# Attention inside a macaron layer: heavy and light key halves take turns within an item, and the values' products come in twos

## The chip, the core and the metric

The kernel runs on one core of a Trainium2 chip. The metric is device microseconds of one execution, the median of several runs. PE is TensorE (its weight loads are listed as PEld), DVE is VectorE, ACT is ScalarE, POOL is GpSimd, SP issues DMAs.

## What is computed

A macaron layer over 16 sequences of 512 rows of 128 values: half a feed-forward layer with routed experts, attention, and half a feed-forward layer again. The change is in attention alone, of which this much matters:

```python
q, k, v = proj(Wq, bq), proj(Wk, bk), proj(Wv, bv)              # 16 heads of 8 values
dist = clip(arange(s)[:, None] - arange(s)[None, :], -128, 128) + 128
scores = einsum('bhqd,bhkd->bhqk', q, k)
scores = scores + einsum('bhqd,qkd->bhqk', q, rel_emb[dist])    # relative positions, clipped at 128
attn = softmax(scores / sqrt(8), axis=-1)
local_ctx = einsum('bhqk,bhkd->bhqd', attn, v)
# a global, linear part (sigma_q, M, z) is mixed in with a gate, then the output projection
```

Within 128 positions the relative term differs from key to key; beyond that it is one number per query on each side. So only blocks of 128 keys next to the block of 128 queries, or equal to it, need a table added; the others get their term inside the score product.

## The kernel before

**Items and steps.** Attention works through 128 items. An item is one sequence (16), one set of four heads (4) and one half of the queries (2 blocks of 128): `half_of(c)` is c % 2, eight items make a sequence (`PER`). The queue of each engine is written out slot by slot, `slot(c)` with four steps k = 0 to 3, and each slot works on several items at once: raw scores of item c + 2, the band product of item c + 4, turned scores of item c.

**One step on PE** (L1437 to L1457), in this order:
- `scores(c + 2, k)` (L1240): for two heads, 128 queries by 512 keys into `ps_s`, for DVE's row maximum (L1838), which adds the table `rel` on the way. A score bank is written again one step later, when its maximum is taken (`max_done`). The heads are the pair 1 - k%2.
- `band_product(c + 4, k)` (L1256): queries by 256 relative positions for the pair k%2. ACT copies it out (L1481), POOL sends it to HBM (L1575, L1577), SP fetches it back skewed into `rel` (L1751). The copies of k = 0 and 2 wait until the transfer of the item before, out of the same half of `src`, has landed.
- `scores_turned(c, k)` (L1212): keys by queries, for two heads and one half of the keys (two blocks of 128), into the two banks of `ps_t`. Each bank waits until ACT has taken the exponential of the step before out of it (`exp_done`).
- `add_turned(c, k)` (L1225): turns the blocks of `rel` and adds them in PSUM, for adjacent blocks only. Of the four pairs of a key block and a query block in a step, all four are adjacent where keys and queries are the same half (8 additions for two heads: a heavy step), and one is where they are not (2 additions: a light step).
- On some steps work of other stages in the bank `misc`: the turn of the maxima (L1312, every k = 0), projections (L1368, L1374, L1390, L1433), groups of four transposes (L1322, L1334, L1407, L1428), smaller products (L1343, L1351, L1382, L1421). Their places (slot in the sequence, k) are fixed in constants.
- `values(..., kb)` (L1270): the products of probabilities and values for one block of 128 keys and four heads, 8 instructions in the trace (two passes each).

**The order of the steps.** `scores_turned` takes key half k // 2 and head pair k % 2. For even items the half of the keys at k = 0 and 1 is the half of the queries, for odd ones it is that at k = 2 and 3: heavy, heavy, light, light, and then light, light, heavy, heavy. The products of the first two key blocks stand behind k = 2 and 3, those of the last two behind k = 0 and 1 of the next slot.

**The others.** ACT per step: the copy of the band product, then two exponentials (L1472), then now and then a copy of a projection. DVE per step: what is due of `maxima_out` (k = 1, L1848), `values_out` (k = 2, L1856), projections, `GLOBAL_OUT` and the like, `route_low` (L2073); then two maxima; then small steps of the router.

Of the kernel before, what the change touches and what calls it, by code (L numbers as in the profile page):

```python
# [5 lines left out]
P = 128  # L6
# [955 lines left out]
def attention_phase(nc, io, X, STATS, tables, rows):  # L962
# [4 lines left out]
    QPB = 4  # L967
    S = QPB * P
    B = Q // QPB
    HG = 4  # L970
# [45 lines left out]
    with ExitStack() as ctx:  # L1016
# [6 lines left out]
        def ring(name, per):  # L1023
            return Ring(ctx.enter_context(nc.semaphore(f"at_{name}")), per)
# [67 lines left out]
        m_turned, m_row = ring("m_turned", 1), ring("m_row", 1)  # L1092
        m_in = [ring(f"m_in{r}", 16) for r in range(R2)]
        t_done, exp_done = ring("t_done", 2 * HG), ring("exp_done", 2 * HG)
        pv_done, oc_done = ring("pv_done", QPB), ring("oc_done", 1)
        o_turned, o_step = ring("o_turned", QPB), ring("o_step", 2 * QPB)
        g_prod, g_step = ring("g_prod", 2), ring("g_step", 6)
        mixed_done, mixed_turned, mixedT_done = (ring(x, 1) for x in ("mixed_done", "mixed_turned", "mixedT_done"))
# [68 lines left out]
        def set_of(c):  # L1167
            return c % PER // 2

        def par_of(c):  # L1170
            return c // PER % R2

# [25 lines left out]
        def _(pe):  # L1198
            def scores_turned(c, k):

                j, r, s, kp, hp = c, par_of(c), set_of(c), k // 2, k % 2
                if k == 0:
                    m_ring, n = pair_ring(m_in, c)
                    pe.wait_ge(m_ring.sem, m_ring.at(n, 16))
                for i in range(2):
                    h = 2 * hp + i
                    exp_done.wait(pe, j, 2 * k + i - 1)
                    rows = slice(32 * h, 32 * h + ROW + 1)
                    q = qs[rows, r, s, HALF * half_of(c):HALF * (half_of(c) + 1)]
                    for n in range(2):  # L1210
                        kb = 2 * kp + n
                        pe.matmul(ps_t[:, i, HALF * n:HALF * (n + 1)], ks[rows, r, s, kb * P:(kb + 1) * P], q,  # L1212
                                  start=(n == 0), stop=False, skip_group_check=True)

            def add_turned(c, k):

                kp, hp = k // 2, k % 2
                for i in range(2):
                    for n in range(2):
                        kb = 2 * kp + n  # L1220
                        for l in range(2):
                            qb = 2 * half_of(c) + l
                            if kb < qb - 1 or kb > qb + 1:
                                continue
                            ins = pe.matmul(ps_t[:, i, HALF * n + P * l:HALF * n + P * (l + 1)],  # L1225
                                            rel[:, c % RREL, l, 2 * hp + i, kb * P:(kb + 1) * P], ident[:],
                                            start=False, stop=True, is_transpose=True, skip_group_check=True)
                    ins.then_inc(t_done.sem, 1)

# [26 lines left out]
                    ins = pe.matmul(ps_r[:, i, 0:BAND], qs[rows, r, s, rows_of(c, l)], rs[rows, :], start=True, stop=True)  # L1256
                ins.then_inc(qr_done.sem, 1)

            def values(c, kb):

                j, r, s = c, par_of(c), set_of(c)
                pe.wait_ge(exp_done.sem, exp_done.at(j, HG * (kb // 2 + 1)))
                if kb == 0:
                    oc_done.wait(pe, j, 0)
                    if c % PER == 0:
                        b = c // PER
                        pe.wait_ge(v_done.sem, v_done.at(b, 1))
                for g in range(HG):
                    at = (HG * s + g) * (HD + 1)
                    ins = pe.matmul(ps_v[32 * g:32 * g + 32, 0:HALF], v[:, r, kb, at:at + 32],  # L1270
                                    probs[:, kb // 2, g, kb % 2, :], start=(kb == 0), stop=(kb == QPB - 1),
                                    skip_group_check=True)
                ins.then_inc(pv_done.sem, 1)

            def maximum_left(c):
# [160 lines left out]
            def slot(c):  # L1436
                for k in range(4):  # L1437
# [13 lines left out]
                        project(c, k)  # L1451
                    if leaving(c) is not None:
                        leave(c, k)
                    if k < 2 and item(c - 1) is not None:
                        values(c - 1, 2 + k)
                    elif k >= 2 and item(c) is not None:
                        values(c, k - 2)  # L1457
            for c in SLOTS:
                slot(c)

# [1 line left out]
        def _(act):  # L1462
            def exponent(c, k):

                j, kp, hp = c, k // 2, k % 2
                if k == 0:
                    pv_done.wait(act, j, 2 - QPB)
                elif k == 2:
                    pv_done.wait(act, j, 0)
                for i in range(2):  # L1470
                    act.wait_ge(t_done.sem, t_done.at(j, 2 * k + i + 1))
                    act.activation(probs[:, kp, 2 * hp + i].rearrange("p n q -> p (n q)"), ps_t[:, i, :],  # L1472
                                   ACT.Exp).then_inc(exp_done.sem, 1)

            def band_out_of_psum(c, k):
# [346 lines left out]
        def _(dve):  # L1822
# [27 lines left out]
            def values_out(c):  # L1850

                j, b = c, leaving(c)
                dve.wait_ge(pv_done.sem, pv_done.at(j, QPB))
                if c % PER < 2 and b is not None:
                    dve.wait_ge(o_turned.sem, o_turned.at(b, 2 * (c % PER) + 2))
                dve.tensor_copy(oc[:, 2 * half_of(c):2 * half_of(c) + 2, set_of(c), :],  # L1856
                                ps_v[:, 0:HALF].rearrange("p (t q) -> p t q", t=2)).then_inc(oc_done.sem, 1)
# [550 lines left out]
```

## Time and profile before

| | |
|---|---|
| median of 3 runs | 2129.41 us (2128.08 to 2130.55) |
| the profiled execution | 2133.66 us, its span 2131.9 us |
| attention, first to last scores on PE | 451.4 to 1745.1 us of the span |
| PE / DVE / ACT / POOL busy | 91% / 71% / 64% / 60% of the span |
| mean granted TensorE clock | 0.934 of 2.4 GHz |

The rest of the span is the two feed-forward layers. In the timeline a row is a run of like instructions: where the first starts, how long the run takes until its last one ends, the engine, the line, what is written from what, how many, and in brackets the idle time of the engine just before. Matmuls overlap, so the time of a stage on PE is read from the start of its row to the start of the next. A step of PE goes from the start of one row of L1240 to the start of the next.

### The profile page before, as it was taken

The page shows a single profiled execution, that of the slowest core. Times are in us where ns is not written, and L with a number is a line of the kernel's source. Part 1 is how long each engine was busy: PE and PEld are TensorE (multiplying, and loading weights), DVE is VectorE, ACT ScalarE, POOL GpSimd, SP SyncE. Part 2 cuts the span into 40 slices and gives each one's busy share as a digit, 9 for nine tenths or more (in the row PEclk, how much of TensorE's full clock was granted, in tenths as well). Part 3 has the DMA queues.
Part 4 walks back from the last instruction along what each step waited for, and adds up shares of the span by engine and source line. Part 5 has one row for each costly group of instructions (what it writes and reads, how often), then busy time and mean ns, then how long its engine had stood idle before and what let it go on. Part 6 is the DMA issues. An engine that isn't in the chain of part 4 may idle for free. (4 is left out here: it accounts for less than half of the span.)

```text
span 2131.9 us, 47704 instructions
## 1 busy us (share of the span) xinstructions
PE 1947.8 (91%) x15256; PEld 1345.7 (63%) x15256; DVE 1507.4 (71%) x4387; ACT 1370.2 (64%) x2645; POOL 1272.4 (60%) x1806
## 2 busy tenths in 40 slices
PE   4779999769999999999999999999999996899992
PEld 3667788535666666665666666666666664688882
DVE  7987667646767767777767677777777664876775
ACT  3767677536766766667766666766766652667771
POOL 0777217346656656776766667666676442637775
PEclk9999999859999989899989999999999897999996
DMA  5457889688989888888888888888888751277757
GB/s 145 170 206 265 290 258 307 197 214 253 255 236 263 238 233 255 217 240 255 231 241 240 220 249 253 238 247 240 238 256 239 212 150 62 82 234 265 256 194 253
DMA packets 291741, 484.75 MB, mean 227 GB/s; under 512 B 42724, under 2 KB 198500, under 8 KB 291492
## 3 DMA queue, kind: packets, MB, share of 16 engines
q1 hardware_dynamic: 234612, 298.65, 49.2%
q0 software_dynamic: 54144, 181.91, 26.5%
q8 instruction: 124, 2.03, 0.4%
q10 hardware_dynamic: 2736, 1.13, 0.2%
q14 instruction: 125, 1.02, 0.2%
HBM read 245.23 MB, written 208.89 MB: 213 GB/s over the span
## 5 line engine op out<-in xcount | busy, mean ns | idle before, releaser
L1838 DVE CUSTOM_DVE_ANT_0 at_junk<-at_ps_s,at_rel 128x512 bf16<-128x512 f32 x1024 | 664.2, 686 | 190.7 <-PE at_ps_s L1240 166.4
L1472 ACT ACTIVATE at_probs<-at_ps_t 128x512 f32<-128x512 f32 x1024 | 559.1, 599 | 81.9 <-PE at_ps_t L1225 70.6
L1481 ACT COPY at_src<-at_ps_r 128x512 f32<-128x512 f32 x512 | 302.0, 590 | 376.5 <-PE at_ps_r L1256 265.6
L1225 PE MATMUL at_ps_t<-tab_ident,at_rel 128*128 128x128 f32 x2560 | 412.3, 294 | 0.0
L1270 PE MATMUL at_ps_v<-at_probs,at_v 128*32 128x256 f32 x4096 | 340.8, 406 | 0.2 <-ACT at_probs L1472 0.2
L1240 PE MATMUL at_ps_s<-at_ks,at_qs 31*128 31x512 f32 x1024 | 326.2, 515 | 11.3 <-DVE at_mx L1838 6.2
L1225 PEld LDWEIGHTS at_ps_t<-tab_ident,at_rel 128*128 128x128 f32 x2560 | 284.8, 146 | 72.2 <-issue 9.1
L1240 PEld LDWEIGHTS at_ps_s<-at_ks,at_qs 31*128 31x128 f32 x1024 | 124.8, 188 | 267.0 <-DVE at_mx L1838 150.6
L1212 PE MATMUL at_ps_t<-at_qs,at_ks 32*128 32x256 f32 x2048 | 271.3, 300 | 5.1 <-DMA at_qs<-at_mrow 2.2
L645 POOL DMA_INDIRECT rows_x<-ffn_sent_or_back,rows_index x160 | 168.1, 1051 | 145.3 <-ACT ffn_sent_or_back L596 97.7
L912 DVE TENSOR_TENSOR ffn_h<-ffn_silu,ffn_ps_gate 128x512 f32<-128x512 f32 x234 | 160.4, 686 | 129.5 <-ACT ffn_silu L615 129.1
L615 ACT ACTIVATE ffn_silu<-ffn_ps_mid 128x512 f32<-128x512 f32 x234 | 139.5, 596 | 173.3 <-PE ffn_ps_gate L443 173.3
L1256 PE MATMUL at_ps_r<-tab_rs,at_qs 31*128 31x256 f32 x1024 | 205.4, 398 | 22.5 <-ACT at_src L1481 15.8
L1212 PEld LDWEIGHTS at_ps_t<-at_qs,at_ks 32*128 32x128 f32 x2048 | 207.8, 194 | 26.2 <-ACT at_probs L1472 19.5
L1575 POOL DMA_DIRECT2D at_band<-at_src x192 | 142.3, 741 | 108.6 <-POOL at_src L1568 107.1
L652 POOL DMA_INDIRECT rows_t<-ffn_y,ffn_row_ids x156 | 152.3, 977 | 79.5 <-issue 45.4
L1567 POOL COPY at_far<-at_src 128x4 f32<-128x4 f32 x192 | 37.0, 193 | 233.9 <-ACT at_src L1481 233.6
L850 DVE TENSOR_TENSOR ffn_h_lo<-ffn_h,ffn_h_hi 128x512 fp32r<-128x512 f32 x234 | 160.2, 685 | 0.1
L1270 PEld LDWEIGHTS at_ps_v<-at_probs,at_v 128*32 128x32 f32 x4096 | 82.3, 110 | 103.3 <-issue 53.9
L561 ACT CAST ffn_h_hi<-ffn_h 128x512 fp32r<-128x512 f32 x234 | 143.2, 612 | 2.6 <-DVE ffn_h L912 2.6
L443 PE MATMUL ffn_ps_mid<-ffn_xT_hi,ffn_w_expert 128*128 128x512 f32 x340 | 135.9, 400 | 5.5 <-issue 3.6
L1856 DVE COPY at_oc<-at_ps_v 128x256 f32<-128x256 f32 x128 | 54.2, 423 | 120.6 <-PE at_ps_v L1270 120.5
(295 smaller groups left out, 3775.8 us busy)
## 6 DMA issues: line engine op xcount, KB each, us to landing
at_band<-at_src POOLq DMA_DIRECT2D x192, 574.0 KB
at_rel<-at_band SPq DMA_DIRECT2D x512, 143.5 KB
ffn_w_expert<-rows_w SPq DMA_DIRECT2D x85, 768.0 KB, 4.7
at_band<-at_src POOLq DMA_DIRECT2D x64, 512.0 KB
ffn_xg<-rows_x SPq DMA_DIRECT2D x46, 256.0 KB
rows_y<-ffn_y SPq DMA_DIRECT2D x46, 256.0 KB, 5.8
ffn_xg<-rows_x SPq DMA_DIRECT2D x39, 258.0 KB
at_rel<-at_band SPq DMA_DIRECT2D x64, 128.0 KB
```

Of the source, the lines that this page charges most:

```text
L645: pool.indirect_dma_start(to, bass.IndirectOffsetOnAxis(index[:, t // PAIR, k, t % PAIR * T + s, :], 0), xe[:, i % RX, k, s, :], None).the ...
L652: pool.indirect_dma_start(rows.t, bass.IndirectOffsetOnAxis(row_ids[:, b % RI, c, :], 0), y[:, b % RY, c, :], None).then_inc(z_out[b % RY] ...
L850: dve.tensor_tensor(h_lo[:, u % RH, :], h[:, u % RH, :], h_hi[:, u % RH, :].bitcast(F32), ALU.subtract).then_inc(hlo_done, 1)
L912: dve.tensor_tensor(h[:, u % RH, :], silu[:, u % RH, :], ps_gate[:, u % 2, :], ALU.mult).then_inc(h_done, 1)
L1212: pe.matmul(ps_t[:, i, HALF * n:HALF * (n + 1)], ks[rows, r, s, kb * P:(kb + 1) * P], q, start=(n == 0), stop=False, skip_group_check=True)
L1225: ins = pe.matmul(ps_t[:, i, HALF * n + P * l:HALF * n + P * (l + 1)], rel[:, c % RREL, l, 2 * hp + i, kb * P:(kb + 1) * P], ident[:], sta ...
L1240: pe.matmul(ps_s[:, i, :], qs[rows, r, s, rows_of(c, l)], ks[rows, r, s, :], start=True, stop=True).then_inc(s_done.sem, 1)
L1256: ins = pe.matmul(ps_r[:, i, 0:BAND], qs[rows, r, s, rows_of(c, l)], rs[rows, :], start=True, stop=True)
L1270: ins = pe.matmul(ps_v[32 * g:32 * g + 32, 0:HALF], v[:, r, kb, at:at + 32], probs[:, kb // 2, g, kb % 2, :], start=(kb == 0), stop=(kb == ...
L1472: act.activation(probs[:, kp, 2 * hp + i].rearrange("p n q -> p (n q)"), ps_t[:, i, :], ACT.Exp).then_inc(exp_done.sem, 1)
L1481: act.copy(src[:, l, 2 * hp:2 * hp + 2, 0:BAND], ps_r[:, :, 0:BAND]).then_inc(qr_out.sem, 1)
L1838: dve.tensor_tensor_reduce(out=junk[:, i, :], in0=ps_s[:, i, :], in1=rel[:, c % RREL, l, h, :], scale=1.0, scalar=-3e38, op0=ALU.add, op1= ...
```

## The change

Within an item, the steps now go through one pair of heads and both halves of the keys, then through the other pair. `unit` gives the half of the keys and the head: the half of the queries first (heavy), then the other (light). The half `k % 2` of `probs` now holds heavy or light steps. The products are called twice an item, each time for both blocks of a key half: those of the heavy steps behind k = 3, those of the light ones behind k = 0 of the next slot. `pv_done` counts two an item instead of four, and the waits on it follow. The exponentials of k = 0 and k = 1 wait for the products of the item before that read the same half of `probs`.

```diff
+        def unit(c, k, i):
+            return (half_of(c) + k) % 2, 2 * (k // 2) + i
...
             def scores_turned(c, k):
-                j, r, s, kp, hp = c, par_of(c), set_of(c), k // 2, k % 2
+                j, r, s = c, par_of(c), set_of(c)
...
                 for i in range(2):
-                    h = 2 * hp + i
+                    kp, h = unit(c, k, i)
                     exp_done.wait(pe, j, 2 * k + i - 1)
...
             def add_turned(c, k):
-                kp, hp = k // 2, k % 2
                 for i in range(2):
+                    kp, h = unit(c, k, i)
...
-            def values(c, kb):
+            def values(c, part):
                 j, r, s = c, par_of(c), set_of(c)
-                pe.wait_ge(exp_done.sem, exp_done.at(j, HG * (kb // 2 + 1)))
-                if kb == 0:
+                pe.wait_ge(exp_done.sem, exp_done.at(j, 2 * HG - 2 + 2 * part))
+                if part == 0:
                     oc_done.wait(pe, j, 0)
...
-                for g in range(HG):
-                    at = (HG * s + g) * (HD + 1)
-                    ins = pe.matmul(ps_v[32 * g:32 * g + 32, 0:HALF], v[:, r, kb, at:at + 32],
-                                    probs[:, kb // 2, g, kb % 2, :], start=(kb == 0), stop=(kb == QPB - 1),
-                                    skip_group_check=True)
+                for n in range(2):
+                    for g in range(HG):
+                        kp, _ = unit(c, part, 0)
+                        at = (HG * s + g) * (HD + 1)
+                        ins = pe.matmul(ps_v[32 * g:32 * g + 32, 0:HALF], v[:, r, 2 * kp + n, at:at + 32],
+                                        probs[:, part, g, n, :], start=(part == 0 and n == 0), stop=(part == 1 and n == 1),
+                                        skip_group_check=True)
                 ins.then_inc(pv_done.sem, 1)
...
-                    if k < 2 and item(c - 1) is not None:
-                        values(c - 1, 2 + k)
-                    elif k >= 2 and item(c) is not None:
-                        values(c, k - 2)
+                    if k == 0 and item(c - 1) is not None:
+                        values(c - 1, 1)
+                    elif k == 3 and item(c) is not None:
+                        values(c, 0)
...
             def exponent(c, k):
-                j, kp, hp = c, k // 2, k % 2
-                if k == 0:
-                    pv_done.wait(act, j, 2 - QPB)
-                elif k == 2:
-                    pv_done.wait(act, j, 0)
+                j = c
                 for i in range(2):
+                    _, h = unit(c, k, i)
                     act.wait_ge(t_done.sem, t_done.at(j, 2 * k + i + 1))
-                    act.activation(probs[:, kp, 2 * hp + i].rearrange("p n q -> p (n q)"), ps_t[:, i, :],
+                    if i == 0 and k < 2:
+                        pv_done.wait(act, j, k - 1)
+                    act.activation(probs[:, k % 2, h].rearrange("p n q -> p (n q)"), ps_t[:, i, :],
                                    ACT.Exp).then_inc(exp_done.sem, 1)
...
             def values_out(c):
-                dve.wait_ge(pv_done.sem, pv_done.at(j, QPB))
+                dve.wait_ge(pv_done.sem, pv_done.at(j, 2))
```

## Rows read from the trace of the kernel before

**Rows 1.** The page: busy us, share, instructions; then one costly group (busy, mean ns).

```profile
PE 1947.8 (91%) x15256; PEld 1345.7 (63%) x15256; DVE 1507.4 (71%) x4387; ACT 1370.2 (64%) x2645; POOL 1272.4 (60%) x1806
...
L1270 PE MATMUL at_ps_v<-at_probs,at_v 128*32 128x256 f32 x4096 | 340.8, 406 | 0.2 <-ACT at_probs L1472 0.2
```

**Rows 2.** Windows: stretch, length, busy us by engine, PEclk, DMA share, GB/s.

```profile
521.00:1702.10 1181.10, 1152.78 (x10846) 732.19 (x10843) 844.90 (x2786) 795.90 (x1490) 781.89 (x1273) 0.95 0.85 241
...
1427.60:1446.10 18.50, 18.00 (x145) 11.58 (x141) 10.19 (x33) 10.57 (x20) 11.55 (x20) 0.72 0.77 216
```

**Rows 3.** The tile of the scores: durations min/median/max in ns, first and last start.

```profile
L1240 PE MATMUL at_ps_s<-at_ks,at_qs x1024: 488/497/792, 451.4 to 1745.1; 31*128 31x512 f32 x171
```

**Rows 4.** Timeline of PE from 562.71 to 567.31: two heavy steps.

```profile
562.71 1.09 PE L1225 MATMUL at_ps_t<-tab_ident,at_rel 128*128 128x128 f32 x8
...
564.59 0.64 PE L1270 MATMUL at_ps_v<-at_probs,at_v 128*32 128x256 f32 x8
565.16 0.50 PE L1240 MATMUL at_ps_s<-at_ks,at_qs 31*128 31x512 f32 x2
565.17 0.39 PE L1256 MATMUL at_ps_r<-tab_rs,at_qs 31*128 31x256 f32 x2
565.39 0.40 PE L1212 MATMUL at_ps_t<-at_qs,at_ks 32*128 32x256 f32 x4
565.72 1.09 PE L1225 MATMUL at_ps_t<-tab_ident,at_rel 128*128 128x128 f32 x8
566.74 0.64 PE L1270 MATMUL at_ps_v<-at_probs,at_v 128*32 128x256 f32 x8
567.31 0.50 PE L1240 MATMUL at_ps_s<-at_ks,at_qs 31*128 31x512 f32 x2
```

**Rows 5.** Timeline of PE, ACT and DVE from 1347.44: the run of light steps.

```profile
1347.44 1.09 PE L1225 MATMUL at_ps_t<-tab_ident,at_rel 128*128 128x128 f32 x8
...
1348.14 1.09 ACT L1472 ACTIVATE at_probs<-at_ps_t 128x512 f32<-128x512 f32 x2
...
1348.90 0.64 PE L1270 MATMUL at_ps_v<-at_probs,at_v 128*32 128x256 f32 x8
...
1349.47 0.50 PE L1240 MATMUL at_ps_s<-at_ks,at_qs 31*128 31x512 f32 x2
...
1350.03 0.44 PE L1225 MATMUL at_ps_t<-tab_ident,at_rel 128*128 128x128 f32 x2
1350.08 0.59 ACT L1481 COPY at_src<-at_ps_r 128x512 f32<-128x512 f32 x1 [0.86 <-PE at_ps_r L1256]
...
1350.40 0.64 PE L1270 MATMUL at_ps_v<-at_probs,at_v 128*32 128x256 f32 x8
...
1350.72 0.69 DVE L1838 CUSTOM_DVE_ANT_0 at_junk<-at_ps_s,at_rel 128x512 bf16<-128x512 f32 x1
1350.97 0.99 PE L1240 MATMUL at_ps_s<-at_ks,at_qs 31*128 31x512 f32 x2
...
1351.47 0.18 PEld L1240 LDWEIGHTS at_ps_s<-at_ks,at_qs 31*128 31x128 f32 x1 [0.32 <-DVE at_mx L1838]
...
1353.52 1.10 PE L1240 MATMUL at_ps_s<-at_ks,at_qs 31*128 31x512 f32 x2 [0.38 <-DVE at_mx L1838]
...
1355.74 0.50 PE L1240 MATMUL at_ps_s<-at_ks,at_qs 31*128 31x512 f32 x2
...
1358.49 0.50 PE L1240 MATMUL at_ps_s<-at_ks,at_qs 31*128 31x512 f32 x2
```

**Rows 6.** Waits: engine, line, whom it waited for, us in total, times, longest.

```profile
PEld at_ps_s L1240 <- DVE at_mx L1838: 150.6, 366, 1.1
...
ACT at_src L1481 <- DMA at_band<-at_src: 108.9, 74, 2.9
```

**Rows 7.** Timeline of PE: two steps of a later run at the lower clock.

```profile
1437.57 0.79 PE L1240 MATMUL at_ps_s<-at_ks,at_qs 31*128 31x512 f32 x2
...
1441.65 0.79 PE L1240 MATMUL at_ps_s<-at_ks,at_qs 31*128 31x512 f32 x2
```

## What the change is predicted to do

> **What bounds the kernel now.** I read the page first: PE is busy 91% of the span, DVE, ACT and POOL 60 to 71% [rows 1]. The reader should see that PE is the engine nearest to full. The windows view of the middle of attention puts numbers to it: PE busy 1152.78 of 1181.1 us, granted clock 0.95 [rows 2]. With two levels, 2.4 and 1.2 GHz, 0.95 means that some 10% of that stretch, about 118 us, ran at the lower one. The view of the tile that takes the scores gives the pace: first scores at 451.4, last at 1745.1 us, 512 steps [rows 3], so (1745.1 - 451.4)/511 = 2.53 us a step and 10.13 us an item. The other two phases (the two feed-forward layers) are not touched, so the sum is made per item and taken 128 times.
>
> "Busy" hides the waits, so I read the timeline by the starts of the steps. A heavy step with nothing extra (8 turned additions, L1225) runs 565.16 to 567.31: 0.56 to the additions, 1.02 for them, 0.57 for the products, 2.15 us [rows 4]. A light one (2 additions) runs 1349.47 to 1350.97: 0.56 + 0.37 + 0.57 = 1.50 us [rows 5]. Two of each are 7.30. The work on `misc` comes on top: a projection adds 0.86 (562.71 to 564.59 is 1.88, less 1.02) [rows 4], four transposes 0.44 (1347.44 to 1348.90 is 1.46, less 1.02) [rows 5]. Counting four projections, seven groups of four transposes, eight turns of the maxima and the smaller products of a sequence by these gives about 10.6 us for eight items, 1.3 an item (an estimate). So 7.3 + 1.3 = 8.6 would be work, and 1.5 us of an item's 10.13 are waits and slow clock.
>
> Where they lie: before the change an even item runs heavy, heavy, light, light and an odd one light, light, heavy, heavy, so four light steps stand in a row. In the row shown they start at 1349.47, 1350.97, 1353.52, 1355.74 and the next heavy one at 1358.49: 1.50, 2.55, 2.22, 2.75 us [rows 5]. The light step is too short for the engines behind PE. Scores issued at 1349.47 let the next second score in at 1351.47 only, after DVE's second maximum (1350.72 plus 0.69): 2.00 us from step to step, whatever PE does [rows 5]. The list of waits has the same: PE's loads idle 150.6 us for that maximum, 366 times [rows 6]. In such runs the clock also falls: the same two places of another sequence, 1437.57 and 1441.65, lie 4.08 us apart where 1355.74 to 1358.49 took 2.75 [rows 5, 7], and the window around them has a granted clock of 0.72 [rows 2]. That is 1.33 us per 4.08 at the lower level, a third; 118 us then cost some 39 us, 0.30 an item. A third wait is ACT's for the band transfer, 108.9 us, 74 times [rows 6].
>
> **The change part by part.** **The order** becomes heavy, light, heavy, light in every item. No instruction is added or removed except semaphore steps, and of the queues only PE's own order changes; DVE, ACT, POOL and SP keep theirs. ACT's new wait for `pv_done` stands behind its wait for `t_done`; PE issues the products it asks for before the additions of that step, so it is up already: nothing. `values_out` needs products now done after the 1st step instead of the 2nd, and the products' own wait for it moves from the 3rd step to the 4th: both looser.
>
> **Products in twos.** One group of 8 takes 0.57 and its two waves lie 0.24 apart (0.64 for the group [rows 4], 0.41 for one product [rows 1]); sixteen should take 0.57 + 2 x 0.24 = 1.05. Against 2 x 0.57 that is 0.09 less, twice an item. From additions straight to scores no row exists: the passage from additions to products is inside the 1.02 and 0.37 above, and I take the same (bounds 0.1 less and 0.1 more, twice an item, 26 us either way in all).
>
> **Heads.** Scores use the head pair 1 - k%2, the band product k%2, the turned scores so far k%2 and now k//2. In the rows scores and band start together (565.16, 565.17) and the turned scores follow at 565.39, when 256 columns of the band are through but the 512 of the scores are not [rows 4]: other heads, other rows of the array, side by side. In the 2nd and 3rd step the turned scores now share heads with the scores. Cost between 0 and one band's length, 0.11 each (half of 0.22); I take 0.11 in the 2nd and find it hidden in the 3rd. The Trainium skill ("TensorE: Matmul & The Clock Gate", Part 3, "The mechanism") says that loads run beside matmuls only in other row groups; by that alone, with nothing hiding it, both steps would pay, some 28 us in all, where my sum has 14.
>
> **The cover that goes.** Products stood between each step's additions and the next step's turned scores, and hid exponentials and maxima. The 2nd and 3rd step lose it. I follow one item from the start of its 2nd step (light):
> - Additions at 0.67, PE free at 1.04 (plus `misc` work). The copy starts 0.61 after the scores and takes 0.59 (1350.08 after 1349.47), then the two exponentials 1.09: done at 2.29. DVE lets the second score in at 2.00 [rows 5]. The second turned score can go at 2.34, additions follow 0.44 later: 2.78. So PE waits 0.7 to 1.2 us, but 0.44 of `misc` work, which most 2nd steps have, costs nothing there.
> - Heavy additions 2.78 to 3.80. The exponentials start 0.70 after them and end 1.09 later (1347.44, 1348.14) [rows 5], so the second turned score of the 4th step goes at 4.61 and its additions at 5.05, against 4.36 without a wait: 0.7 lost, or nothing where the 3rd step has 0.86 of `misc` work (mean 5.07).
> - Light additions 0.37, `misc` work 0.43 (four of eight items have a piece of 0.86 here), sixteen products 1.05: the next item starts at 6.92. Its 1st step is 0.56 + 1.02 + 0.11 + 1.05 = 2.75, long enough for DVE and ACT.
>
> The sum is 9.67 us, 0.46 under 10.13. What stalls still: two places of eight items where DVE has a chain of its own ahead of the maxima (`GLOBAL_OUT`, `route_low`; the second is the loss of the step at 1350.97, 2.55 long) some 0.5 each, 0.13 an item; and of the 0.30 for the clock I keep a third, 0.10, since no two light steps are neighbours now but PE still idles twice an item. That makes 9.90, 0.23 less, times 128 is 29 us. The profiled execution took 2133.66 us (span 2131.9) and the median is 2129.41, within 0.2%; I take the 29 us from the median: **2100 us**.
>
> **The rivals.**
> - **Everything lines up**: no falls and no chains, 9.67 an item, 59 us less: 2070. For it: waits of ACT for the band fall in steps with slack. Chance 0.18.
> - **The clock doesn't recover**: what helps PE to the upper level may not be the additions. The falls then stay at 0.30, the 0.13 too, 9.67 + 0.43 = 10.10: 2126, no change. Against it, the fall shown comes in a run of steps with 2 additions each, while steps with 8 ran at full clock [rows 4, 7]. The Trainium skill (same page, "Part 4: PE-mode transpose") says that transposes don't count as activity for the clock; by that, mixing heavy steps in would not help. The rows of the light run disagree. The same time would come if the band's round trip (ACT's 108.9 us [rows 6]) sets the pace. Chance 0.12.
> - **The lost cover costs the clock** (the slower side): PE now idles about 0.7 us behind the 2nd step and, in the four of eight items without `misc` work in the 3rd, 0.7 again. Two such waits in a row are what preceded the fall in the light run (steps of 2.55 and 2.22 in place of 1.50) [rows 5, 7]. If the clock falls in those 64 items, at 1.33 each [rows 5, 7], 85 us are added to 9.67 + 0.13: 2129 - 59 + 17 + 85 = 2172. It decides from about 30 such items on, where 9.67 + 0.13 + 0.31 reaches 10.13. Chance 0.22.
> - That the order isn't carried out can't be: each engine's queue is written out.
>
> **How the numbers follow.** Forecast 2100 (2085 to 2120), chance 0.48; 0.18 for 2070, 0.12 for 2126, 0.22 for 2172. Less than 0.2% is about what a measurement of this kernel can't tell from no change. The uncertain passage (26 us either way) blurs all of them. Faster 0.67: the first two and a little of the third; same 0.09; slower 0.24. The range 2060 to 2165 leaves out the better edge of the first rival and the worse half of the last.
>
> **What would show it.** Right: in the trace of after 16 products take about 1.05 us; a light step without products is followed by scores some 2.0 us after its own and by heavy additions 2.1 us after the light ones; the 4th step's additions start about 2.3 us after the 3rd's; scores start 9.9 us apart item by item; the granted clock in the middle is 0.97 or more, and ACT's wait for the band shrinks. Wrong: additions to scores far from 0.2 us, a clock under 0.95, a copy for the band that waits in the 3rd step and holds up the exponentials, or steps 2 and 3 that take over 5.1 us from scores to the 4th step's additions.

## The result and the profile after

The changed kernel takes 2145.43 us (median of 6 runs, 2139.61 to 2154.32) beside 2129.64 us for the kernel before (6 runs): a ratio of 1.0085, 95% interval 1.0049 to 1.0120. It is slower by some 18 us, where 2100 us was forecast. The profiled execution took 2147.03 us, its span is 2145.2.

The page of the changed kernel: busy time by engine, and the group of the products (busy, mean ns).

```profile
PE 1960.4 (91%) x15256; PEld 1405.2 (66%) x15256; DVE 1508.5 (70%) x4387; ACT 1367.0 (64%) x2645; POOL 1271.3 (59%) x1806
...
L1275 PE MATMUL at_ps_v<-at_probs,at_v 128*32 128x256 f32 x4096 | 285.7, 398 | 0.1
```

The same instructions, and the products are busy 55.1 us less than in [rows 1]. The windows view of the middle of attention:

```profile
521.00:1702.10 1181.10, 1152.15 (x10768) 777.82 (x10771) 841.64 (x2770) 788.54 (x1483) 779.13 (x1269) 0.96 0.86 240
```

The tile of the scores, with first and last start:

```profile
L1244 PE MATMUL at_ps_s<-at_ks,at_qs x1024: 488/497/792, 455.0 to 1756.8; 31*128 31x512 f32 x171
```

The granted clock is 0.96 after 0.95, PE is as busy as in [rows 2], and the scores take 1301.8 us from first to last where [rows 3] gives 1293.7. Of 13.3 us that the span grew, 8.1 lie here; 3.6 lie ahead of the first scores (455.0 after 451.4) and 1.6 behind the last, in layers that the change doesn't touch. The list of waits (us in total, times, longest):

```profile
ACT at_src L1485 <- DMA at_band<-at_src: 147.1, 113, 4.0
...
PEld at_ps_s L1244 <- DVE at_mx L1842: 102.1, 315, 1.8
PEld at_ps_r L1260 <- ACT at_src L1485: 33.6, 31, 2.4
PEld at_ps_t L1216 <- ACT at_probs L1476: 29.1, 118, 1.7
```

PE waits less for DVE's maxima than in [rows 6] (102.1 for 150.6 us), ACT more for the band (147.1 for 108.9 us). The places at which PE waits show in the timeline: first the four steps of an item of the kernel before, the sixth of its sequence, in which nothing was late. The rows are the starts of its steps (first scores), and of the next item's.

```profile
1257.96 0.51 PE L1240 MATMUL at_ps_s<-at_ks,at_qs 31*128 31x512 f32 x2
...
1259.57 0.99 PE L1240 MATMUL at_ps_s<-at_ks,at_qs 31*128 31x512 f32 x2
...
1261.67 0.68 PE L1240 MATMUL at_ps_s<-at_ks,at_qs 31*128 31x512 f32 x2
...
1264.30 0.50 PE L1240 MATMUL at_ps_s<-at_ks,at_qs 31*128 31x512 f32 x2
...
1266.61 0.50 PE L1240 MATMUL at_ps_s<-at_ks,at_qs 31*128 31x512 f32 x2
```

Light, light, heavy, heavy: 1.61, 2.10, 2.63, 2.31, together 8.65 us. The same item of the changed kernel, PE and its loads (PEld):

```profile
1264.61 0.50 PE L1244 MATMUL at_ps_s<-at_ks,at_qs 31*128 31x512 f32 x2
...
1264.84 0.40 PE L1216 MATMUL at_ps_t<-at_qs,at_ks 32*128 32x256 f32 x4
...
1266.30 1.07 PE L1275 MATMUL at_ps_v<-at_probs,at_v 128*32 128x256 f32 x16
1267.30 0.50 PE L1244 MATMUL at_ps_s<-at_ks,at_qs 31*128 31x512 f32 x2
...
1267.64 0.40 PE L1216 MATMUL at_ps_t<-at_qs,at_ks 32*128 32x256 f32 x4
...
1268.59 1.11 PE L1244 MATMUL at_ps_s<-at_ks,at_qs 31*128 31x512 f32 x2
...
1269.20 0.18 PEld L1244 LDWEIGHTS at_ps_s<-at_ks,at_qs 31*128 31x128 f32 x1 [0.43 <-DVE at_mx L1842]
...
1269.96 1.09 PE L1229 MATMUL at_ps_t<-tab_ident,at_rel 128*128 128x128 f32 x8
1270.99 0.50 PE L1244 MATMUL at_ps_s<-at_ks,at_qs 31*128 31x512 f32 x2
...
1271.79 0.29 PEld L1216 LDWEIGHTS at_ps_t<-at_qs,at_ks 32*128 32x128 f32 x2 [0.20 <-ACT at_probs L1476]
...
1272.22 0.44 PE L1229 MATMUL at_ps_t<-tab_ident,at_rel 128*128 128x128 f32 x2
1272.59 1.07 PE L1275 MATMUL at_ps_v<-at_probs,at_v 128*32 128x256 f32 x16
1273.59 0.50 PE L1244 MATMUL at_ps_s<-at_ks,at_qs 31*128 31x512 f32 x2
```

Heavy, light, heavy, light: 2.69, 1.29, 2.40, 2.60, together 8.98 us. From scores to additions takes 0.56 where nothing waits [rows 4]; here it takes 1.37 in the 3rd step and 1.23 in the 4th: 0.81 and 0.67 us of waiting, for DVE's maxima, then for ACT's exponentials.

To compare whole kernels I read the starts of these rows for 112 items (14 sequences) out of each trace. A **clean item** is the mean over the eight places of a sequence of the length that one item in five at that place stays under: it leaves out most of what a late band and a low clock add. "Waits" are, in the same way, what a step takes from scores to additions above 0.56; "products" is the time from the first product of a group to the next scores. The mean is over all items from the ninth on.

| kernel, run | ratio (95%) | waits in step 1, 2, 3, 4 | products | clean item | mean item |
|---|---|---|---|---|---|
| before | 1 | 0.11, 0.25, 0.06, 0.26 | 2.33 | 9.48 | 10.18 |
| after | 1.0085 (1.0049 to 1.0120) | 0.10, 0.11, 0.58, 0.50 | 2.00 | 9.67 | 10.22 |
| before, all in twos | 1.0106 (1.0036 to 1.0175) | 0.05, 0.02, 0.42, 0.59 | 2.00 | 9.59 | 10.12 |
| before, first half in twos | 1.0082 (1.0049 to 1.0114) | 0.05, 0.26, 0.07, 0.54 | 2.14 | 9.64 | 10.09 |
| before, second half in twos | 0.9948 (0.9908 to 0.9988) | 0.11, 0.01, 0.39, 0.20 | 2.19 | 9.39 | 9.96 |
| after, products by heads | 1.0305 (1.0235 to 1.0375) | 0.11, 0.11, 0.18, 0.00 | 3.93 | 10.54 | 10.59 |

A clean item grew by 9.67 - 9.48 = 0.19 us, times 128 is 24 us. Waits went up by 0.61 and products down by 0.33; 0.09 came off the rest. The means come from single executions (that of before took 2133.66 us, over its median), so the ratios decide which kernel is faster, and the clean items say where.

### The profile page after: what moved, and what is told of

Same layout as the page of the kernel before. It is cut to its first block and busy times, and to the rows that moved or that the text cites. A ratio compares the mean times of both kernels' runs of the same rounds, so it can differ in the third digit from the quotient of the medians.

```text
span 2145.2 us, 47704 instructions
## 1 busy us (share of the span) xinstructions
PE 1960.4 (91%) x15256; PEld 1405.2 (66%) x15256; DVE 1508.5 (70%) x4387; ACT 1367.0 (64%) x2645; POOL 1271.3 (59%) x1806
## 3 DMA queue, kind: packets, MB, share of 16 engines
q14 instruction: 125, 1.02, 0.2%
## 5 line engine op out<-in xcount | busy, mean ns | idle before, releaser
L1229 PE MATMUL at_ps_t<-tab_ident,at_rel 128*128 128x128 f32 x2560 | 405.8, 291 | 0.0
L1216 PE MATMUL at_ps_t<-at_qs,at_ks 32*128 32x256 f32 x2048 | 326.4, 307 | 5.3 <-ACT at_probs L1476 3.2
L1229 PEld LDWEIGHTS at_ps_t<-tab_ident,at_rel 128*128 128x128 f32 x2560 | 280.4, 144 | 72.0 <-issue 7.1
L1275 PE MATMUL at_ps_v<-at_probs,at_v 128*32 128x256 f32 x4096 | 285.7, 398 | 0.1
L1216 PEld LDWEIGHTS at_ps_t<-at_qs,at_ks 32*128 32x128 f32 x2048 | 247.5, 192 | 47.2 <-ACT at_probs L1476 29.1
L645 POOL DMA_INDIRECT rows_x<-ffn_sent_or_back,rows_index x160 | 166.6, 1041 | 147.1 <-ACT ffn_sent_or_back L596 99.9
L1275 PEld LDWEIGHTS at_ps_v<-at_probs,at_v 128*32 128x32 f32 x4096 | 109.8, 112 | 101.4 <-issue 41.6
L443 PE MATMUL ffn_ps_gate<-ffn_xT_hi,ffn_w_expert 128*128 128x512 f32 x340 | 134.7, 396 | 0.0
```

What stands on the lines that cost most here:

```text
L443: ins = pe.matmul(out, lhs(a), rhs(b), start=start and i == 0, stop=stop and i == 2)
L645: pool.indirect_dma_start(to, bass.IndirectOffsetOnAxis(index[:, t // PAIR, k, t % PAIR * T + s, :], 0), xe[:, i % RX, k, s, :], None).the ...
L1275: ins = pe.matmul(ps_v[32 * g:32 * g + 32, 0:HALF], v[:, r, 2 * kp + n, at:at + 32], probs[:, part, g, n, :], start=(part == 0 and n == 0) ...
```

## The experiments

**One part alone: the order of before, all products in twos.** Theory: the products no longer cover DVE and ACT behind the 2nd and 3rd step. Rivals: the new order of the steps costs, or the late band.

```diff
...
-                    if k < 2 and item(c - 1) is not None:
-                        values(c - 1, 2 + k)
-                    elif k >= 2 and item(c) is not None:
-                        values(c, k - 2)
+                    if k == 0 and item(c - 1) is not None:
+                        values(c - 1, 1)
+                    elif k == 3 and item(c) is not None:
+                        values(c, 0)
...
```

> One part of the change alone: the order of the steps stays that of before (heavy, heavy, light, light and back), but the products come in groups of sixteen behind the 4th and the 1st step. If the products in twos are what costs (steps 2 and 3 lose their cover, and the light steps still stand in a row), this is slower than before by more than the whole change is: 2150 us or more. If the order with light steps between heavy ones is what costs, this is at 2130 or below, since two drains an item are saved, some 0.35 us of products by the trace of after. By the sum that the prediction used, an item is 9.54 us here without other waits, 0.13 under that of the whole change.

Measured: 2147.66 us, ratio 1.0106 (1.0036 to 1.0175), a little under the 2150 expected. The products alone cost as much as the whole change; the order of the steps, on top of them, adds nothing that can be told here.

**The light pairs exchanged, so that turned scores and scores share no heads in the 2nd step.** They still share them in the 3rd, and now in the 4th too.

```diff
-            return (half_of(c) + k) % 2, 2 * (k // 2) + i
+            return (half_of(c) + k) % 2, 2 * ((k + 1) // 2 % 2) + i
```

> The whole change, but the light steps take the two pairs of heads the other way round (pairs 0, 1, 1, 0 instead of 0, 0, 1, 1), so that turned scores and raw scores no longer share heads in the 2nd step, only in the 3rd and 4th, where the turned scores wait for exponentials anyway. If shared rows of the array are what costs, 0.11 us in each 2nd step, this is 14 us faster than the whole change (near 2131). If the exponentials behind the copy set the start of the 3rd step's additions, nothing: 2145, within 5.

Measured: 2140.88 us, ratio 1.0069 (1.0037 to 1.0102), not to be told from the change's 1.0085. In its trace the 2nd step's wait of 0.11 is gone, but the 3rd step waits 0.65 where it waited 0.58, and a clean item is 9.65 after 9.67.

**The band without its pad, in the changed kernel and in the one before.** GpSimd's copy of the pad and the wait behind it stand between ACT's copy and the transfer. The wait alone is, in the list of waits of the kernel before:

```profile
POOL at_band L1575 <- POOL at_src L1568: 107.1, 191, 0.9
```

Without copy and wait the band leaves earlier: by the traces the issue of a padded band starts 1.03 us (median) behind the end of ACT's copy in both kernels, and 0.30 us without the pad, so 0.73 us earlier; the columns of the pad keep what the prologue wrote, so a part of the scores differs.

```diff
...
-                if padded:
-                    edge = src[:, l, :, BAND - 1:BAND]
-                    pool.tensor_copy(far[:, c % RREL, l], edge).then_inc(pad_done.sem, 1)
-                    pool.tensor_copy(src[:, l, :, BAND:WIDE], edge.broadcast_to([P, HG, PAD])).then_inc(pad_done.sem, 1)
...
+                pool.dma_start(heads[:, :, PAD:PAD + BAND], src[:, l, :, 0:BAND]).then_inc(band_out[l].sem, 16)
                 if padded:
-                    pool.wait_ge(pad_done.sem, pad_done.at(j // 2, 4 * half_of(c) + 2 * l + 2))
-                    pool.dma_start(heads[:, :, PAD:HEADW], src[:, l]).then_inc(band_out[l].sem, 16)
-                else:
-                    pool.dma_start(heads[:, :, PAD:PAD + BAND], src[:, l, :, 0:BAND]).then_inc(band_out[l].sem, 16)
+                    pool.tensor_copy(far[:, c % RREL, l], src[:, l, :, BAND - 1:BAND]).then_inc(pad_done.sem, 1)
...
```

> The whole change, with a shorter way of the band product: the pad of 31 columns a head is left out (it stays zero, so scores far from the diagonal next to the band's edge are not the reference's), and POOL issues the transfer right after ACT's copy instead of two copies and a wait later, some 0.8 us earlier. Theory: the change is slower because ACT's copy in the 3rd step waits for that transfer, and with it exponentials and turned scores that no products cover any more. Then this gains 25 to 45 us: 2100 to 2120, ACT's wait for the band falls from 147 to under 90 us and the steps of the fifth item of a sequence lose their long 4th step. Rival, the lost cover by itself (exponentials and maxima, whatever the band does): within 8 us of the whole change. Second rival, the clock alone: the wait falls but the time stays, with the same share at the lower clock.

> The same shortening in the kernel before (the pad left out, the transfer 0.8 us earlier). Theory: before, products cover part of what the band's wait holds up, so this gains less than the whole change does by it, some 10 to 20 us: 2110 to 2120, and then the whole change without the pad is no slower than this. If the gain is the same in both, the band's wait costs alike before and after and doesn't explain the 16 us.

Measured: changed 2117.47 us, 0.9974 (0.9945 to 1.0004); before 2088.68 us, 0.9838 (0.9774 to 0.9902). ACT's wait for the band, in the lists of waits of the changed kernel and of the one before:

```profile
ACT at_src L1489 <- DMA at_band<-at_src: 20.1, 21, 2.4
```

```profile
ACT at_src L1485 <- DMA at_band<-at_src: 21.4, 16, 2.0
```

The wait is nearly gone in both, and it gave the kernel before 1.6% (34 us, where 10 to 20 were expected) and the changed one 1.1%. So the theory on record, that the late band costs the changed kernel more, was wrong, though the changed kernel's time came within its range. The band holds up both, so it can't be what makes the change slower: without it the change is still 1.4% behind. Clean items are 9.44 in the kernel before and 9.60 in the changed one.

**All in twos, in the order of before, without the pad.** The first and the third edit together.

> The order of before, all products in twos, and the band's pad left out (its columns keep what the prologue wrote, so part of the scores differs), so that the band leaves about .8 us earlier. It stands against the kernel before without the pad (.9838 of before). Theory (lost cover): the twos cost the same without the band's wait, 15 to 25 us more than that: 2103 to 2115 us, ratio .991 to .997. Rival (the twos cost because they make the band late): the cost is gone without the pad and the .28 us of products saved shows: at or below 2089 us, ratio .970 to .985.

Measured: 2129.05 us, 1.0032 (0.9991 to 1.0072), against 0.9838 without the twos. It came out above what was expected: the twos cost 2% here, some 40 us, and a clean item is 9.64 beside 9.44, which is 26 of them. The cost doesn't come by way of the band. The rest goes with the clock. The windows view of the middle, in the order of before without the pad, first with the products in eights, then all in twos:

```profile
521.00:1702.10 1181.10, 1161.53 (x11354) 740.28 (x11354) 878.60 (x2916) 829.29 (x1552) 762.61 (x1130) 0.98 0.85 239
```

```profile
521.00:1702.10 1181.10, 1142.55 (x10987) 770.41 (x10986) 862.69 (x2824) 811.43 (x1512) 749.83 (x1116) 0.96 0.84 235
```

The same holds run by run: the granted clock of the whole execution is 0.944 to 0.952 with eights (4 runs) and 0.929 to 0.943 with twos (10 runs), and time at the lower clock grows from 0.43 to 0.90 us an item, 0.64 of it in the 4th step. In the changed kernel without the pad it is 0.29 us an item, at 0.945 to 0.955 (10 runs). So in the order of before the lost cover costs the clock too, and the new order spares that. Beside the changed kernel without the pad (0.9974) the new order gains about 0.6%, which is as large as the two intervals together.

**Only the first half's products in twos, or only the second's**, in the order of before:

```diff
-                    elif k >= 2 and item(c) is not None:
-                        values(c, k - 2)
+                    elif k == 3 and item(c) is not None:
+                        values(c, 0)
+                        values(c, 1)
```

```diff
-                    if k < 2 and item(c - 1) is not None:
-                        values(c - 1, 2 + k)
+                    if k == 0 and item(c - 1) is not None:
+                        values(c - 1, 2)
+                        values(c - 1, 3)
```

> The kernel before, its order of steps kept, with only the products of the first key half put together: both blocks (16 products) behind the 4th step, none behind the 3rd; the second half's stay in eights behind the 1st and 2nd step. Theory (lost cover): against before, the run with all products in twos shows the weight-load stalls of the 4th step up by .35 us an item (.34 to .69) and of the 2nd kind of step after a bare one up alike; of the first half's move .35 falls to the bare 3rd step, .07 comes back in the 1st step, and .14 is saved on the products: +.14 us x 128 items = +18 us, ratio 1.006 to 1.011, nearly the whole of what all products in twos cost. Rival (band wait and clock, a cost that each grouping brings alike): about half of 1.0106, 1.005 here and in the other half's run. Rival 2 (16 products in a row are slow in themselves): 1.005 in both as well, with sixteen above 1.14 us.

> The kernel before with only the second key half's products put together: 16 behind the next item's 1st step, none behind its 2nd; the first half's stay in eights behind the 3rd and 4th. Theory (lost cover): the bare 2nd step costs .36 us an item at the 3rd, the fuller 1st step gives .26 back at the 2nd, .14 is saved on the products: -.04 us x 128 = -5 us, ratio .995 to 1.000. Rivals (a cost that each grouping brings alike): 1.005.

Measured: first half 2137.12 us, 1.0082 (1.0049 to 1.0114); second half 2115.18 us, 0.9948 (0.9908 to 0.9988), the only part of the change that gains. Both as the theory had it (the second just at the edge of its range), and the rivals' equal halves fall. The timeline of the run with the first half in twos, the 3rd and 4th step (both heavy) of an item that is again the sixth of its sequence:

```profile
1493.93 0.69 PE L1240 MATMUL at_ps_s<-at_ks,at_qs 31*128 31x512 f32 x2
...
1494.97 1.09 PE L1225 MATMUL at_ps_t<-tab_ident,at_rel 128*128 128x128 f32 x8
1495.99 0.50 PE L1240 MATMUL at_ps_s<-at_ks,at_qs 31*128 31x512 f32 x2
...
1496.86 0.29 PEld L1212 LDWEIGHTS at_ps_t<-at_qs,at_ks 32*128 32x128 f32 x2 [0.20 <-ACT at_probs L1473]
...
1497.29 1.09 PE L1225 MATMUL at_ps_t<-tab_ident,at_rel 128*128 128x128 f32 x8
1498.31 1.07 PE L1270 MATMUL at_ps_v<-at_probs,at_v 128*32 128x256 f32 x16
1499.31 0.50 PE L1240 MATMUL at_ps_s<-at_ks,at_qs 31*128 31x512 f32 x2
```

The two steps take 5.38 us where the same two took 2.63 + 2.31 = 4.94 in the kernel before. The sixteen products take 1.00 and so save 0.14; but 4th-step additions that follow the scores by 1.30 lose 0.74. With products behind the 3rd step that loss is 0.16 (the step of before at 1264.30: 2.31 less 0.56, 1.02 and 0.57), and 0.74 - 0.16 - 0.14 is the 0.44. The first half's products can't leave the 3rd step for nothing; the second half's leave the 2nd step at the price of 0.33 in the 3rd, get 0.24 back in the 2nd because the longer 1st step covers it, 0.06 in the 4th, and save 0.14.

**Cover given back to the changed kernel: products by heads.** The two probability halves of `probs` allow nothing earlier than the 4th step for whole blocks of the first half. By heads they do: the four products of a step's two heads go behind the next step. A second buffer of probabilities, which would allow whole blocks, wasn't tried.

```diff
...
                 for n in range(2):
-                    for g in range(HG):
-                        kp, _ = unit(c, part, 0)
+                    for i in range(2):
+                        kp, g = unit(c, step, i)
...
                     if k == 0 and item(c - 1) is not None:
-                        values(c - 1, 1)
-                    elif k == 3 and item(c) is not None:
+                        values(c - 1, 3)
+                    if k == 2 and c % PER == 2 and item(c) is not None:
                         values(c, 0)
+                    if k > 0 and (k, c % PER) != (1, 2) and item(c) is not None:
+                        values(c, k - 1)
...
```

> The changed kernel with its order of steps, but the values' products by heads, 8 split into fours: the four of a step's two heads (both blocks of one key half) behind the next step, so that every step has a piece behind it again; the copy of the products out of PSUM one step earlier on VectorE. Theory (lost cover): the stalls of the changed kernel are about .62 us in the 3rd and .5 us in the 4th step; a piece of some .5 us (if fours take half of eights' pass twice over) behind the 2nd and 3rd step takes .4 to .5 of each away, the 2nd and 1st step lose .2 to .3, the products cost 2.0 to 2.3 us an item in place of 2.0: -.3 to -.6 us an item, 2070 to 2107 us, ratio .976 to .993. Rival (the order of steps itself, or the band and the clock, cost the time): no better than before, 1.000 to 1.010.

Measured: 2188.83 us, ratio 1.0305 (1.0235 to 1.0375). The time expected was missed by far, and by one term. The windows view of that run:

```profile
521.00:1702.10 1181.10, 1178.51 (x10420) 745.57 (x10421) 823.96 (x2680) 763.81 (x1432) 757.89 (x1230) 1.00 0.82 232
```

Its waits for the maxima and the exponentials:

```profile
PEld at_ps_s L1244 <- DVE at_mx L1844: 42.5, 107, 2.6
PEld at_ps_t L1216 <- ACT at_probs L1478: 5.1, 15, 0.9
```

Its timeline of PE, one piece of products and the scores behind it:

```profile
1260.68 1.06 PE L1275 MATMUL at_ps_v<-at_probs,at_v 128*32 128x256 f32 x8
1261.66 0.56 PE L1244 MATMUL at_ps_s<-at_ks,at_qs 31*128 31x512 f32 x2
```

Eight product rows over two heads take 0.98 us, where eight over four heads take 0.57 and sixteen over four take 1.00. So products cost 3.93 us an item, 1.93 more. But the wait in the 3rd step falls from 0.58 to 0.18 and in the 4th from 0.50 to nothing, and the clock of the stretch is 1.00. That fits the theory's half: give nearly every step a piece behind it, and the waits and the slow clock go. It is no proof by itself, since steps that are longer for any reason also leave DVE and ACT more time. The version is no use, since the pieces cost more than they hide.

**A faster way for the band, with everything computed.** The table of the band product gets columns that repeat its last one, so that PE makes the pad and the band leaves right behind ACT's copy:

```diff
...
-                    ins = pe.matmul(ps_r[:, i, 0:BAND], qs[rows, r, s, rows_of(c, l)], rs[rows, :], start=True, stop=True)
+                    wide = WIDE if half_of(c) == 0 or l == 0 else BAND
+                    ins = pe.matmul(ps_r[:, i, 0:wide + wide % 2], qs[rows, r, s, rows_of(c, l)], rs[rows, 0:wide + wide % 2], start=True, stop=True)
...
```

> The kernel before, whole, with the band's pad made by TensorE: the table of the band product has 32 more columns that repeat its last one, so the product and ScalarE's copy are 287 wide where a pad is needed, GpSimd's copy of the pad (0.29 us and the 0.55 us wait behind it) goes, and the band leaves right behind ScalarE's copy; the copy of the far column follows the transfer. Theory (the band's round trip is in the way before and after alike): leaving the pad out gained 1.6% in the kernel before (2089 us); this costs ScalarE some 0.04 us a copy and TensorE 31 columns a product, so nearly all of it comes: ratio .980 to .990. Rival (it was the smaller transfer, 256 in place of 287 columns, that gained): .995 to 1.000.

> The changed kernel, whole, with the band's pad made by TensorE. Theory (lost cover, which the band has no part in): it gains about 1.1% as it did without the pad, to .995 to 1.001 of before, and stays 1 to 1.6% behind the kernel before with the same edit. Rival (the change costs because its band comes late): it closes up to the kernel before with the same edit.

> The same, and the second key half's products alone in twos behind the 1st step (what gave .9948 by itself). Theory (cover and band are two separate causes, and their gains add up): .974 to .985, 2066 to 2090 us, below both the kernel before and the changed one, and below the run with the pad by TensorE alone. Rival (the second half's gain was a gain on the band's wait): no faster than the pad by TensorE alone.

Measured: before 2092.39 us, 0.9836 (0.9789 to 0.9884); changed 2107.90 us, 0.9920 (0.9892 to 0.9947); before with the second half in twos **2071.10 us, 0.9777 (0.9710 to 0.9843)**. The first and the last are within what the theory expected, the changed kernel came a little better than its 0.995. The transfer is as large as ever, so it was its start and not its size. The changed kernel stays 0.9% behind the one before with the same edit (1 to 1.6% expected). The last version beats both kernels. That it also beats the pad by TensorE alone is less sure: their intervals overlap, and clean items, 9.33 beside 9.49, speak for it. In the last version GpSimd's timeline of one band, and the wait for it, read:

```profile
1496.41 0.76 POOL L1578 DMA_DIRECT2D at_band<-at_src  x1 [0.86 <-ACT at_src L1489]
1497.10 0.28 POOL L1579 COPY at_far<-at_src 128x4 f32<-128x4 f32 x1
```

```profile
ACT at_src L1489 <- DMA at_band<-at_src: 14.3, 15, 2.1
```

## Why the prediction was wrong, step by step

- **The chain through the changed item: right.** In the item shown the second score of the 3rd step goes 1.90 us after the scores of the 2nd (2.00 predicted), heavy additions at 2.66 (2.78), those of the 4th step 2.26 later (2.27), sixteen products take 1.00 (1.05). A clean item is 9.67 us, which is the sum of the prediction; with parts up to 0.12 off, that it fits to the last digit is luck.
- **The step that failed: "The sum is 9.67, 0.46 under 10.13".** It set a clean item of after against a mean item of before. The same chain was never followed through the kernel before. There a clean item is 9.48 us: it waits 0.68 us in its four steps where the changed one waits 1.29, and 0.33 less for products doesn't make up for that. On equal terms the sum is 0.19 us *over*, 24 us, and the measured 18 us (ratio 1.0049 to 1.0120, 10 to 26 us) agree with that.
- **The term mis-sized: "What stalls still", 0.23.** In the traces a mean item lies above a clean one by 10.18 - 9.48 = 0.70 before and by 10.22 - 9.67 = 0.55 after. In the prediction's own terms that is the whole miss: 9.67 and 0.55, not 0.23, come to 10.22, no less than before. So almost half of the "1.5 us of waits and clock" was what disturbs some items and not others, and the change keeps most of it. A large part goes with the band: without the pad the two differences are 0.28 and 0.31. The forecast put nothing for the band in the kernel after, while its base still had it; it expected ACT's wait for it to shrink, and that grew (147.1 for 108.9 us).
- **The passage from additions to scores: right.** In the changed item it takes 1270.99 - 1269.96 = 1.03, in the run with the first half in twos 1495.99 - 1494.97 = 1.02, as with products behind it.
- **Shared heads: right in size and place, and hidden.** In the light 2nd step turned scores start 0.34 after the scores, 0.23 in the 1st: the 0.11 that was taken. The Trainium skill ("TensorE: Matmul & The Clock Gate", Part 3, "The mechanism") says that loads run beside matmuls in other row groups; this row agrees. But exchanging the pairs gave nothing certain, since the 3rd step waits for DVE anyway. The prediction said that its sum holds 14 us for this; it holds none, since in its own chain DVE lets the second score of the 3rd step in at 2.00, with the 0.11 or without.
- **The clock: it stayed where it was.** It didn't recover to the 0.97 forecast (0.96 after 0.95 in the traces). Low-clock time is 0.96 us an item in the trace of before and 0.75 in that of after, 0.44 of it in the 4th step. But that trace of before is one of its kernel's slowest-clocked: 0.934 for the whole execution, where its 19 runs beside the first experiments average 0.942 and the changed kernel's 6 runs 0.941. So neither the gain that was forecast nor a fall shows, and the slowdown is not the clock's. In the trace of before the low clock did lie where the prediction put it: 1.67 of the 1.94 us of two items fall in the four light steps and the one behind them. With the run broken up it falls elsewhere, in the changed kernel mostly in the 3rd and 4th step of even items (0.96 of 1.48 us). One sign that the prediction named for being wrong, a late copy for the band that holds up the exponentials, is in the trace, here in a 4th step:

```profile
1260.04 0.50 PE L1244 MATMUL at_ps_s<-at_ks,at_qs 31*128 31x512 f32 x2
...
1260.29 0.59 ACT L1485 COPY at_src<-at_ps_r 128x512 f32<-128x512 f32 x1 [1.24 <-DMA at_band<-at_src]
1260.77 1.09 ACT L1476 ACTIVATE at_probs<-at_ps_t 128x512 f32<-128x512 f32 x2
...
1260.93 0.38 PE L1260 MATMUL at_ps_r<-tab_rs,at_qs 31*128 31x256 f32 x2 [0.39 <-ACT at_src L1485]
1261.43 0.99 PE L1216 MATMUL at_ps_t<-at_qs,at_ks 32*128 32x256 f32 x4
1262.35 0.44 PE L1229 MATMUL at_ps_t<-tab_ident,at_rel 128*128 128x128 f32 x2
```

  ACT's copy waits 1.24 us for the transfer, the exponentials queue behind it, and both PE's band product and its turned scores wait for ACT: 2.31 us from scores to additions in place of 0.56.
- **The rivals.** "The lost cover costs the clock" had the place and the sign, at a price of 1.33 us in 64 items; what is paid in the changed kernel is 0.52 us more waiting in the 3rd step and 0.24 in the 4th of a clean item, and the clock of its runs is that of before. In the order of before without the pad the twos did cost clock as well (0.43 to 0.90 us an item at the lower one). The band holds up both kernels, so it doesn't make the difference. That the run of light steps is what costs, on which the forecast itself rested, was not borne out: with all products in twos the order of before is no slower than the new one beyond what the runs can tell (1.0106 beside 1.0085).
- **Open:** whether the new order by itself gains. The two pairs of runs that differ in it alone give 0.2% and 0.6% in its favour, clean items 0.08 us against it in the one and 0.04 for it in the other; these are about as large as the runs' uncertainty. Without the pad the new order's runs have the higher clock (0.945 to 0.955 beside 0.929 to 0.943). No run has the new order with the products still in eights, since the first half's probabilities are complete only after the 3rd step.

## What to carry to other kernels

Follow one clean item through the kernel before with the same care as through the kernel after, and take the difference of these two; a mean with its disturbances is no base for a clean sum. Work placed between a producer and the engine's next wait on it is cover: before it is moved, ask how long the wait behind it would be without it, and whether the step to which it moves had a wait to hide. Price the parts of a change one by one: here one half gained 0.5% and the other lost 0.8%.

## What the runs showed of the hardware

- Eight products of 32 columns each take 0.57 us over four column groups and 0.98 over two, as long as sixteen over four (1.00): what counts is the number in one group. The Trainium skill ("TensorEngine Tiling (Array Packing)", "Tiling Modes") has four independent tiles of 128 by 32; the rows agree.
- A transfer whose issue moved forward by 0.73 us gained 1.6%, 34 us in 128 items. ACT's wait for it fell from 108.9 us to 21.4. With it went half of the low-clock time of the two traces (0.96 to 0.43 us an item); over all runs the granted clock rose less, from 0.942 to 0.947.
- With a piece of products of about 1 us behind nearly every step PE's granted clock was 1.00 all through the middle of attention, against 0.95 and 0.96, though many of its instructions are the turned additions.
